# Job orders of their own for the periods between layers, and a reordered self layer, filling, drain and end

## What is computed

```python
x = x + _L0_attn_ref(_layernorm(x), ...)         # self attention, 16 heads, softmax
x = x + _L0_xattn_ref(_layernorm(x), ctx, ...)   # cross attention to the context, 16 heads, softmax
x = x + _L0_ffn_ref(_layernorm(x), ...)          # linear layer, weights quantised to 4 bits, plus a rank-16 part
x = x + _L1_attn_ref(_layernorm(x), ...)         # self attention, rms norm, rotary, sigmoid in place of softmax
x = x + _L1_xattn_ref(_layernorm(x), ctx, ...)   # cross attention, one head
x = x + _L1_ffn_ref(_layernorm(x), ...)          # two experts of 64 per chunk of 128 tokens, by a hash of the mean
```

## Time and profile before

| | us |
|---|---|
| median of 3 runs | 1092.66 (1091.53 to 1095.04) |
| the profiled execution's own time | 1096.01 |
| its span, first to last instruction | 1094.2 |
| PE busy | 1020.1 (93%) |
| DVE, ACT, POOL busy | 762.7, 635.6, 583.9 |
| mean granted TensorE clock | 0.977 |

### The profile page before, as it was taken

How to read it: one execution, slowest core, us unless ns; L and a number is a source line. 1 busy time by engine, 2 the same in 40 slices (tenths; PEclk the granted TensorE clock), 3 DMA queues, 4 the chain that set the end, 5 groups by cost and what they waited for, 6 DMA issues and landing times.

```text
span 1094.2 us, 24132 instructions
## 1 busy us (share of the span) xinstructions
PE 1020.1 (93%) x8386; PEld 799.5 (73%) x8386; DVE 762.7 (70%) x1736; ACT 635.6 (58%) x1150; POOL 583.9 (53%) x924
## 2 busy tenths in 40 slices
PE   5679999999987999999999999999999999999967
...
PEclk9689999999998999999999999999999999999988
...
GB/s 205 89 102 82 120 99 79 123 62 79 92 82 68 51 84 80 97 118 93 93 81 81 41 79 73 89 83 81 84 74 91 85 105 64 15 76 166 186 181 197
DMA packets 123484, 104.81 MB, mean 96 GB/s; under 512 B 26826, under 2 KB 123099, under 8 KB 123355
## 3 DMA queue, kind: packets, MB, share of 16 engines
...
...
## 4 chain that ended last, share of the span: by engine, by line
PE 83%; DVE 9%; issue 3%; DMA 2%; ACT 2%; POOL 1%; ACTq 0%; DVEq 0%; SPq 0%; POOLq 0%
PE l_ring L1217 11%; PE l_sT L1132 11%; PE l_o L1152 11%; PE l_copy L1198 9%; PE l_ring L1254 7%; PE l_ring L1167 7%; PE l_ring L1237 4%; PE l_copy L1175 4%; PE l_ring L1874 3%; DVE l_nmax L984 3%; PE l_copy L1152 3%; PE l_ring L1265 2%; PE l_sT L1813 2%; PE l_copy L1245 1%; PE l_o L1846 1%
## 5 line engine op out<-in xcount | busy, mean ns | idle before, releaser
L984 DVE TENSOR_REDUCE l_nmax<-l_ring 128x2 f32<-128x512 f32 (+1 forms) x384 | 250.7, 676 | 104.2 <-PE l_ring L1167 101.4
L763 ACT ACTIVATE l_probs<-l_sT 128x1024 f32<-128x1024 f32 (+1 forms) x256 | 257.8, 1025 | 58.9 <-PE l_sT L1132 45.9
L1132 PE MATMUL l_sT<-qstack,kstack 99*128 99x256 bf16 (+2 forms) x1280 | 187.4, 273 | 0.9 <-ACT l_probs L763 0.5
L1167 PE MATMUL l_ring<-kstack,qstack 96*128 96x256 bf16 (+1 forms) x1024 | 141.5, 247 | 26.7 <-issue 16.3
L1132 PEld LDWEIGHTS l_sT<-qstack,kstack 99*128 99x128 bf16 (+2 forms) x1280 | 125.8, 104 | 25.1 <-issue 2.7
L1167 PEld LDWEIGHTS l_ring<-kstack,qstack 96*128 96x128 bf16 x1024 | 78.1, 98 | 79.2 <-issue 32.0
L1217 PE MATMUL l_ring<-wT,l_zT 128*128 128x256 f32 x512 | 126.8, 386 | 1.7 <-DVE l_attn L1022 0.7
L1152 PE MATMUL l_o<-l_probs,v_heads 128*32 128x256 f32 (+1 forms) x2048 | 127.8, 384 | 0.0
L1198 PE MATMUL l_copy<-l_zT,wT 128*128 128x256 f32 x384 | 104.0, 404 | 4.8 <-ACT l_zT L808 2.8
L1217 PEld LDWEIGHTS l_ring<-wT,l_zT 128*128 128x128 f32 x512 | 92.5, 192 | 14.6 <-issue 2.6
L616 POOL TENSOR_SCALAR factors<-mv 128x2 f32<-128x2 f32 (+1 forms) x77 | 19.4, 253 | 155.8 <-DVE mv L1041 86.4
...
## 6 DMA issues: line engine op xcount, KB each, us to landing
...
kstack<-l_kpart SPq DMA_DIRECT2D x192, 128.0 KB, 4.4
...
```

The lines of the kernel that those rows point to most:

```text
L763: act.activation(probs[buffer_of(g)][0:kp, :], sT[g % 2][0:kp, :], ACT.Sigmoid if sig(u) else ACT.Exp, scale=HD ** -0.5).then_inc(p_ok, 1)
L984: dve.tensor_reduce(nmax[u % 2][:, tt, h0:h0 + hb], bank("s", u, i)[:, 0:hb * sk].rearrange("p (h k) -> p h k", h=hb), AX_X, ALU.max, nega ...
L1132: i = pe.matmul(sT[g % 2][0:kp, j * S:(j + 1) * S], kstack[slot_of(u)][0:rows_used, col * width(u) + kt * kp:col * width(u) + (kt + 1) * k ...
L1167: m = pe.matmul(out[:, j * sk:(j + 1) * sk], qstack[slot_of(u)][0:STACK, (h0 + j) * S + tt * P:(h0 + j) * S + (tt + 1) * P], kstack[slot_o ...
```

## The change

`jobs_of` looks for an order of the period itself before it takes that of the layer:

```diff
-    for word in ORDERS[kind].split():
+    for word in ORDERS.get(f"p{p}", ORDERS[kind]).split():
```

```diff
 ORDERS = {
     "self": """
-        np qa sT0 dq0 s sT1 p0q s qb s s pv2 e0 o1 pv3 e1 p0k s s dq1 ka s kb p1q e2 e3 p2q oT1 sT2 sT3 p1k dk1 dk0 dq2
-        q0 dk2 s va rows vb l2 s lf lo nT qm pv0 p2k o0 pv1 xb s q1 aT s sT4 e4 l1 s s z e5 oT0 sT5 s qA sT6 cl xs w s
-        pa e6 lw xf cx st pb sT7 ws e7 fac s qB""",
+        sT0 p0q qa dq0 s sT1 s qb np s s pv2 e0 pv3 o1 e1 s s ka s kb p0k dk0 p1q oT1 sT2 e2 dq1 p2q dq2 sT3 e3 nT p1k
+        dk1 s p2k dk2 lo l1 l2 va q0 rows vb s pv0 pv1 o0 s aT s s sT4 e4 s z cl e5 oT0 ws qm q1 sT5 s qA sT6 e6 fac xs
+        xb s w pa cx e7 st xf pb s lw lf sT7 qB""",
...
+    "p29": """
+        sT0 p1q ka np kb e0 qa t.w qb s pv2 rope_q o1 dq0 p0q pv3 s sT1 s nT s sT2 oT1 p0k va fr vb pv0 e1 dq2 rope_k
+        aT o0 dk0 p2k s sT3 s dk2 dq1 pv1 cx p2q e2 rows s fz dk1 fxb e3 st pa fst pb qT fac fa fb z oT0 p1k s ffac xb
+        kT cl""",
...
 FILL = (
-    "xs:0 wi dq0:0 xs:1 rows:0 z:0 xf:0 bi xf:1 bv rows:1 qa:0 qb:0 ka:0 p0q:0 p0k:0 kb:0 p1q:0 p1k:0 p2q:0 dq1:0 "
-    "z:1 dk1:0 ka:1 kb:1 dk0:0 qa:1 dk2:0 qb:1 dq2:0 p1q:1 dk0:1 z:2 p2k:0 p1k:1 va:0 dq1:1 dq0:1 p0q:1 p0k:1 xs:2 "
-    "dq2:1 rows:2 p0q:2 dk2:1 l0 dk1:1 vb:0 p2q:1 qa:2 dk0:2 s:0 qb:2 s:0 s:0 s:0 s:0 ka:2 dq0:2 dq2:2 kb:2 p1k:2 "
-    "p2k:1 rows:3 s:0 s:0 dk1:2 s:0 p0k:2 s:0 np:0 s:0 z:3 s:0 p2q:2 s:0 xf:2 dq1:2 s:0 s:0 p1q:2 s:0 s:0 s:1 nT:0 "
-    "s:1 p2k:2 dk2:2")
+    "xf:0 wi xs:0 rows:0 bi xs:1 z:0 xf:1 qa:0 qb:0 bv p0q:0 ka:0 kb:0 dq0:0 p0k:0 dk0:0 dk1:0 rows:1 z:1 p1q:0 "
+    "dq1:0 p1k:0 dk2:0 qa:1 qb:1 p2q:0 dq2:0 p2k:0 dq0:1 p0q:1 ka:1 kb:1 p1q:1 dq1:1 z:2 xs:2 dk0:1 p0k:1 p1k:1 "
+    "rows:2 va:0 dk2:1 vb:0 dq2:1 qa:2 qb:2 s:0 p2k:1 dk1:1 p2q:1 s:0 l0 s:0 s:0 s:0 dq0:2 ka:2 dq2:2 kb:2 rows:3 "
+    "s:0 p1q:2 s:0 s:0 dk0:2 p0k:2 p0q:2 dq1:2 dk1:2 s:0 s:0 s:0 z:3 s:0 p1k:2 s:0 s:0 s:0 s:0 np:0 s:1 nT:0 s:1 "
+    "dk2:2 p2q:2 p2k:2 xf:2")
...
 END = (
-    "t.add:10 t.s:15 t.rows2:13 t.fac:14 t.y:9 t.pT:15 t.out:15 t.fac:15 t.z2:13 t.mean:6 t.hash:6 t.z2:14 "
-    "t.choose:6 t.rows2:14 t.y:10 t.add:11 t.z2:15 t.rows2:15 t.mean:7 t.hash:7 t.choose:7 t.y:11 t.y:12 t.y:13 "
-    "t.fetch:6 t.y:14 t.y:15 t.fetch:7")
+    "t.s:15 t.y:9 t.fac:14 t.rows2:13 t.pT:15 t.z2:13 t.out:15 t.mean:6 t.fac:15 t.hash:6 t.add:10 t.z2:14 "
+    "t.choose:6 t.rows2:14 t.rows2:15 t.z2:15 t.fetch:6 t.add:11 t.y:10 t.mean:7 t.fetch:7 t.hash:7 t.choose:7 "
+    "t.y:11 t.y:12 t.y:13 t.y:14 t.y:15")
```

More of the change, by code:

```diff
@@ new lines @@
+    "p13": """
+        sT0 p0q qa dq0 s sT1 s qb np s s pv2 e0 pv3 o1 e1 s s ka s kb p0k dk0 p1q oT1 sT2 e2 dq1 p2q dq2 sT3 e3 nT p1k
+        dk1 s p2k dk2 lo l1 l2 va q0 rows vb s pv0 pv1 o0 s aT s s sT4 e4 s z cl e5 oT0 ws qm q1 sT5 s qA sT6 e6 fac xs
+        xb s w pa cx e7 st xf pb s lw lf sT7 qB""",
+    "p14": """
+        sT0 p0q qa dq0 s sT1 s qb np s s pv2 e0 pv3 o1 e1 s s ka s kb p0k dk0 p1q oT1 sT2 e2 dq1 p2q dq2 sT3 e3 nT p1k
+        dk1 s p2k dk2 lo l1 l2 va q0 rows vb s pv0 pv1 o0 s aT s s sT4 e4 s z cl e5 oT0 ws qm q1 sT5 s qA sT6 e6 fac xs
+        xb s w pa cx e7 st xf pb s lw lf sT7 qB""",
@@ new lines @@
+    "p15": """
+        sT0 p0q qa dq0 s sT1 s qb np s s pv2 e0 pv3 o1 e1 s s ka s kb p0k dk0 p1q oT1 sT2 e2 dq1 p2q dq2 sT3 e3 nT p1k
+        dk1 s p2k dk2 lo l1 l2 va q0 rows vb s pv0 pv1 o0 s aT s s sT4 e4 s z cl e5 oT0 ws qm q1 sT5 s qA sT6 e6 fac xs
+        xb s w pa cx e7 st xf pb s lw lf sT7 qB""",
+    "p16": """
+        qa sT0 qb s t.w pv2 pv3 e0 p0q sT1 s np p0k ka e1 o1 s kb s rope_k p2k p1q sT2 dq0 oT1 nT p1k fr dk0 va sT3 aT
+        vb s rope_q s dq1 dk1 ffac fst pv0 o0 p2q dq2 fb rows pv1 xb s cx pa e2 pb fxb fac fz z st kT dk2 cl fa qT oT0
+        s e3""",
@@ new lines @@
+    "p28": """
+        np sT0 qa p0q qb t.w s e0 pv2 p0k pv3 s o1 e1 s sT1 ka kb s oT1 sT2 nT va dq0 dk0 dq1 vb dq2 fxb fr s aT p2k
+        sT3 s pv0 cx dk2 pv1 e2 rope_k s dk1 p2q p1q fz pa o0 rows p1k e3 qT pb xb st rope_q cl fa fb oT0 fst kT z s
+        ffac fac""",
+    "p29": """
+        sT0 p1q ka np kb e0 qa t.w qb s pv2 rope_q o1 dq0 p0q pv3 s sT1 s nT s sT2 oT1 p0k va fr vb pv0 e1 dq2 rope_k
+        aT o0 dk0 p2k s sT3 s dk2 dq1 pv1 cx p2q e2 rows s fz dk1 fxb e3 st pa fst pb qT fac fa fb z oT0 p1k s ffac xb
+        kT cl""",
@@ new lines @@
+    "p30": """
+        t.w dq1 sT0 e0 p0k qa p0q e1 qb sT1 pv2 np pv3 s ka p1q kb o1 oT1 p1k nT rope_q s sT2 fr s dk2 sT3 va aT s p2q
+        dq2 p2k rope_k pv0 s vb s fxb rows xb dq0 dk0 fac st e2 pv1 fz pa o0 e3 qT dk1 s pb cx fa z fb kT cl s fst oT0
+        ffac""",
+    "p31": """
+        qa e0 dq1 sT0 t.w p1k sT1 np p0k qb pv2 pv3 s o1 e1 p0q s p2k s ka kb oT1 sT2 fr dq0 sT3 va s rope_q e2 vb
+        rope_k s st aT p2q fxb cx dk0 pv0 dk1 p1q pv1 s xb ffac nT s fz o0 dq2 dk2 fac rows pa pb qT fa fb cl z fst oT0
+        s e3 kT""",
```

46 lines of the change are left out of this document (45 added, 1 removed), and 22 rows, old and new, of tables (DRAIN, FIRST_PERIOD).

## The result

| | before | after |
|---|---|---|
| median of the runs (4 each), us | 1092.78 | 1077.15 (1073.98 to 1077.97) |
| ratio, 95% interval | | 0.9849 (0.9824 to 0.9875) |
| the profiled execution's own time | 1096.01 | 1077.36 |
| its span | 1094.2 | 1075.5 |
| mean granted clock | 0.977 | 0.986 |

The change saves 1.5% of the time, 15.6 us from median to median and 18.7 in the two profiled executions. I had forecast 8.8. The new time lies at the lower end of my range of 1077 to 1091.

A forecast was written before the change was run, and what follows sets the result against it. PE, busy for 93% of the span, was taken as the bound, with gains only where it idles: period 12 5.5, self periods 0, filling 1.5, passage 1.5, end 0.3, in sum 8.8 us, giving 1084 us, range 1077 to 1091.

The forecast's parts named there:

- 4.4 + 0.6: Period 12: new stall of 4.4 us at `nT:13` plus 0.6 for a lower clock, leaving a saving of 5.5 us.
- I take the later release, because the all-reduce stands behind the wait in POOL's queue: Period 12: POOL's block counted from DVE's largest value, POOL free at 334.2 us, a stall of 4.4 us at `nT:13`.
- The count from the copies: Period 12: POOL's block counted from the bias copies' end, POOL free at 331.8 us, a stall of 2.0 us at `nT:13`.
- The rule that I weighed: POOL's all-reduce: first gap of 5.95 us from DVE's value instead of 4.81, saving 1.1 us less; left out of the sum.
- I take 1.5 us won: Filling and first period: q first and an earlier `z:2`, against late transfers of unit 2, save 1.5 us.
- 5 us won (the whole idle time of `z:2`): Filling and first period: upper bound of the gain, PE's wait of 5.09 us at `z:2` going entirely.
- nearest are the rows that stay, I take 0: Ordinary self periods: the nearly unchanged order gains 0 us, with bounds of 3.5 us either way.
- Passage: Period 29: moves on POOL and DVE fill POOL's idle time, 1.5 us won; bounds 3.7 won and 1 lost.
- Drain: Drain: the new order was taken to gain 0 us.
- Tail and end: Tail periods 0; at the end the wait ahead of `z2:15` goes against new delays, 0.3 us won (1.5 won to 1 lost).
- covered entirely: Rival, chance 0.18: period 12 saves 8.5 us and the filling 5, in sum 15.3 us, time 1077 us.

The follow-up runs named there:

- ACT's word alone: Kernel before the change with `z:1` moved ahead of `p1q:0 p1k:0` in FILL, which changes ACT's order alone: 1089.19 us, ratio 0.9961.
- both words alone: Kernel before the change with `z:1` ahead of `p1q:0 p1k:0` and `qa:1 qb:1` ahead of `ka:1 kb:1` in FILL: 1086.69 us, ratio 0.9943.

## Why the prediction was wrong

**Period 12, right in mechanism, short by 2.4 us (7.9 for 5.5, periods 12 and 13 together).** The 8.20 us stall went, and a smaller one stood at `nT:13` for POOL, as forecast. Mis-sized was the new cost: I took 4.4 + 0.6, it was 2.10 and no clock. The step that failed is the choice "I take the later release, because the all-reduce stands behind the wait in POOL's queue". The count from the copies gave 2.0 and was right. In all sixteen kernels with the all-reduce the gap ahead of it is 5.5 to 5.9 us from the end of POOL's last instruction, whether DVE's value comes 0.3 us before that end or 3.7 behind it. So whatever fills the gap runs while POOL waits. The 0.8 us of period 13 I had not seen. The same block was paid somewhere in every order tried: at the first `s` of 12, at `nT:13`, or at the first `s` of 13.

The rule that I weighed (the Trainium skill, GPSIMD Engine Reference, section 2.1 Instruction dispatch: a load of about 6 us at the first call, the wait for an event not part of it) agrees in size; that the wait must be added to it, as I read it, is what these runs refute: with DVE's value 3.7 us behind POOL's last instruction it would give a gap of 9.7, and 5.67 was measured.

**The filling, wrong by 4.5 us (6.0 for 1.5).** The failed steps are "I take 1.5 us won" and its bound, "5 us won (the whole idle time of `z:2`)". I had read the one large wait of DVE and bounded the gain by the one large wait of PE. The cause of most of it lay ahead of both, in ACT's queue: one copy behind a split that waited for POOL, and 2.77 us of waiting on PE that stand in no row I had listed. That word alone gave 5.0 of the 6.0 in its profiled execution and 0.39% (0.23 to 0.55) of the time over ten runs. And I gave the clock no term: the earlier trace rows gave both levels for the same matmul, and the same doubling stood in the filling's x8 groups of 3.75 us. I used it in period 12 only. In the changed kernel it is worth 2.9 us of the 6.0, but 1.6 with ACT's word alone and 0.1 with both words alone; what decides between these is open. `z:2` began at 36.95, not near 41. Right in it: `z:0` is later, by 1.2 us over all executions (1.3 forecast), and PE does wait for the last transfers of unit 2. But those land at 71.3 and not at 75.5 to 77.5, and the wait at `s:2` is 0.7 us here, 0.7 to 2.0 in the nine kernels with the new filling.

**The self list, wrong by 3 us, inside its bound.** The step "nearest are the rows that stay, I take 0" failed. I compared the lists of PE, POOL, DVE and ACT, and not that of SP, where `dk0` stood behind `dk1`; that one word gives the whole gain. Each ordinary period had a wait of some 0.45 us at its first `s` for the last transfer, put down to "issue".

**Passage, right in size by luck** (1.6 for 1.5). I put it on period 29, where POOL's idle time was to be filled; that period became 0.4 us longer, and the gain lies in 28 and 30 to 32. By what wait it came is open. **Drain**: 1.0 won where I took 0, and 0.6 to 1.0 in all nine kernels with the new list. **Tail and end**: 0.3 won forecast, the part alone costs about 0.2% (0.0 to 0.4). That POOL's `add:10` would move into DVE's `choose:6` stood in the prediction; its price didn't.

Of the rivals, "covered entirely" named the size (1077) with half of its reasons: the gap from the copies and a clock that holds, both true, and 5 us in the filling for the whole wait at `z:2`, of which 2.1 were won. In that part it came near by luck.
